# Layer 2 of a two-layer GraphSAGE stage: x·W_r computed beside x·W_l in the projection instead of inside the neighbour sums

## The reference, cut to what matters

```python
def _sage_conv(x, src, tgt, W_l, b_l, W_r):
    n = x.shape[0]
    msgs = x[src]
    agg = jax.ops.segment_sum(msgs, tgt, num_segments=n)
    deg = jax.ops.segment_sum(jnp.ones((src.shape[0],), x.dtype), tgt, num_segments=n)
    agg = agg / jnp.maximum(deg, 1.0)[:, None]
    return agg @ W_l + b_l + x @ W_r
src, tgt = (edge_index[0], edge_index[1])
h = jax.nn.relu(_sage_conv(x, src, tgt, W_l1, b1, W_r1))
logits = _sage_conv(h, src, tgt, W_l2, b2, W_r2)
```

## Time and profile before

| | us |
|---|---|
| median of 3 runs (lowest, highest) | 3331.05 (3328.54, 3333.71) |
| the profiled execution's own time | 3306.88 |
| its span, from first to last instruction | 3304.9 |
| TensorE busy in the span | 2592.2 (78%) |
| VectorE busy | 1966.1 (59%) |
| GpSimd busy | 1819.5 (55%) |
| ScalarE busy | 773.9 (23%) |
| sums of layer 1 | 1913 to 2469 |
| `stage_project` | 2469 to 2511 |
| sums of layer 2 | 2511 to 3069 |

### The profile page before, as it was taken

One profiled execution on the slowest core, in us unless ns is written; L12 is line 12 of the kernel. 1 busy time (PEld: TensorE's weight loads), 2 busy tenths in 40 slices (PEclk: granted clock), 3 DMA queues, 4 the chain that ended last, 5 costly groups with the idle time before them and its releaser, 6 DMA issues. The chain is left out here.

```text
span 3304.9 us, 33972 instructions
## 1 busy us (share of the span) xinstructions
PE 2592.2 (78%) x8449; PEld 1445.8 (44%) x8449; DVE 1966.1 (59%) x4316; ACT 773.9 (23%) x2022; POOL 1819.5 (55%) x1847
## 2 busy tenths in 40 slices
PE   4487784199999899879999877777777777777598
PEld 1133331055544444446666644433334343443476
DVE  7999996377776667514333644444435444444768
ACT  1001010277666666522232300000001000000132
POOL 3777777476665556412100067777754777777310
PEclk8788897599999999989999977788868877777799
DMA  9222220499999999961110033333343333334311
GB/s 256 68 69 82 61 81 13 149 264 263 255 239 234 221 235 234 189 163 49 40 39 9 13 106 105 105 105 105 106 89 101 106 106 105 105 105 103 86 50 41
DMA packets 198569, 401.32 MB, mean 121 GB/s; under 512 B 44315, under 2 KB 93230, under 8 KB 198064
## 3 DMA queue, kind: packets, MB, share of 16 engines
q0 software_dynamic: 93888, 248.27, 31.0%
q1 hardware_dynamic: 98672, 145.05, 13.7%
q10 hardware_dynamic: 5826, 5.93, 0.6%
HBM read 296.76 MB, written 104.52 MB: 121 GB/s over the span
## 5 line engine op out<-in xcount | busy, mean ns | idle before, releaser
L1492 POOL DMA_INDIRECT nbr_yg<-y_d,gidx x878 | 830.1, 945 | 273.0 <-PE nbr_sum L1555 143.6
L1555 PE MATMUL nbr_sum<-nbr_yg,nbr_hot 128*128 128x258 f32 x1756 | 735.3, 534 | 287.3 <-DMA nbr_yg<-y_d,gidx 228.6
L1518 DVE TENSOR_TENSOR nbr<-nbr_sum,nbr 128x258 f32 x878 | 373.5, 425 | 613.4 <-PE nbr_sum L1555 546.7
L1555 PEld LDWEIGHTS nbr_sum<-nbr_yg,nbr_hot 128*128 128x128 f32 x1756 | 367.0, 246 | 643.4 <-DMA nbr_yg<-y_d,gidx 237.7
L704 POOL DMA_INDIRECT qg<-q_d,rb x480 | 470.7, 981 | 322.0 <-DVE hb L787 200.8
L818 PE MATMUL p_sum<-hb,wide 128*96 128x512 f32 x960 | 470.1, 604 | 58.0 <-ACT hb L747 57.1
L362 POOL DMA_INDIRECT recs_d<-recs,slot_src x416 | 403.5, 970 | 152.9 <-issue 135.2
L787 DVE TENSOR_TENSOR hb<-p_h,qg 128x512 f32<-128x512 f32 x480 | 318.3, 684 | 167.1 <-DMA qg<-q_d,rb 156.7
L747 ACT ACTIVATE hb<-hb 128x512 f32<-128x512 f32 x480 | 298.6, 630 | 285.5 <-DVE hb L787 277.5
L566 PE MATMUL acc<-col_hot,lane_hot 128*128 128x440 f16 x832 | 209.9, 419 | 126.8 <-DVE lane_hot L521 126.7
L818 PEld LDWEIGHTS p_sum<-hb,wide 128*96 128x96 f32 x960 | 149.8, 164 | 239.7 <-issue 110.8
(11 more groups left out here) (277 smaller groups left out, 3108.4 us busy)
## 6 DMA issues: line engine op xcount, KB each, us to landing
agg_d<-agg SPq DMA_DIRECT2D x240, 192.4 KB, 5.8
nbr_yg<-y_d,gidx POOLq DMA_INDIRECT x878, 2.7
p_low<-p_d SPq DMA_DIRECT2D x11, 768.0 KB, 13.1
recs_d<-fill SPq DMA_DIRECT2D x16, 510.0 KB, 17.4
rb<-recs_d SPq DMA_DIRECT2D x60, 136.0 KB
qg<-q_d,rb POOLq DMA_INDIRECT x480
recs_d<-recs,slot_src POOLq DMA_INDIRECT x416
agg_d<-no_sums SPq DMA_DIRECT2D x1, 6540.8 KB, 58.5
```

The costliest lines, as they stand in the source:

```text
L1492: pool.indirect_dma_start(yg[t % YB][:, 0:D], None, S.y[:, :], bass.IndirectOffsetOnAxis(ap=C.gidx[:, t:t + 1], axis=0)).then_inc(s_gath[t ...
L1518: dve.tensor_tensor(nbr, p_sum[t % SUMS][:, 0:W], nbr, ALU.add).then_inc(s_acc, 1)
L1555: pe.matmul(p_sum[t % SUMS][:, 0:W], hot[t // BT % HOTS][:, t % BT, :], yg[t % YB][:, :], start=True, stop=True).then_inc(s_sum, 1)
```

## The change

The products x·W_r and the bias of layer 2 leave `stage_neighbours(..., 1)`. `stage_project` loads W_l and W_r side by side into one tile `w_lr` of 512 columns, and for each node tile its two matmuls are 512 columns wide and fill a whole PSUM bank: y in columns 0 to 255, z in columns 256 to 511. A third matmul adds the bias to the right half. VectorE copies the left half out as before; ScalarE copies the right half to `C.z` in a new step `kept`, which waits for `out.empty`, that is for VectorE's copy of the same bank. In ScalarE's order `kept(t - 1)` stands between the relu of tile t+1 and the turned copy of tile t. TensorE waits for `s_z` besides `out.empty` before it fills a bank again. Layer 1 is as it was.

```diff
--- before.py
+++ after.py
@@ -1371,18 +1371,20 @@
     with ExitStack() as ctx:
         m = Mem(nc, ctx, "project_")
         HB, XB, YB = 3, 3, 4
-        w_l, rdeg = m.sb("w_l", [P, KD, D]), m.sb("rdeg", [P, NT, 1])
+        w_lr, b_r, rdeg = m.sb("w_lr", [P, KD, 2 * D]), m.sb("b_r", [1, D]), m.sb("rdeg", [P, NT, 1])
         h = [m.sb(f"h{b}", [P, D]) for b in range(HB)]
         x = [m.sb(f"x{b}", [P, D]) for b in range(XB)]
         y = [m.sb(f"y{b}", [P, D]) for b in range(YB)]
         tr, out = Ring(m, "turn", 3), Ring(m, "out", 3)
-        s_w, s_deg, s_h, s_x = (m.sem(n) for n in ("w", "deg", "h", "x"))
+        s_w, s_deg, s_h, s_x, s_z = (m.sem(n) for n in ("w", "deg", "h", "x", "z"))
         s_yst = [m.sem(f"yst{b}") for b in range(YB)]
 
         with nc.Block() as block:
             @block.sync
             def _(sp):
-                sp.dma_start(w_l[:, :, :], rows_on_partitions(A.W_l2)).then_inc(s_w, 16)
+                sp.dma_start(w_lr[:, :, 0:D], rows_on_partitions(A.W_l2)).then_inc(s_w, 16)
+                sp.dma_start(w_lr[:, :, D:2 * D], rows_on_partitions(A.W_r2)).then_inc(s_w, 16)
+                sp.dma_start(b_r[:, :], A.b2.rearrange("(a n) -> a n", a=1)).then_inc(s_w, 16)
                 for t in range(NT):
                     sp.wait_ge(out.empty, t + 1)
                     sp.dma_start(S.y[t * P:(t + 1) * P, :], y[t % YB][:, :]).then_inc(s_yst[t % YB], 16)
@@ -1423,13 +1425,20 @@
                         act.wait_ge(tr.full, t - XB + 1)
                     act.activation(x[t % XB][:, :], h[t % HB][:, :], ACT.Relu).then_inc(s_x, 1)
 
+                def kept(t):
+                    act.wait_ge(out.empty, t + 1)
+                    act.activation(C.z[:, t, :], out.banks[t % len(out.banks)][:, D:2 * D], ACT.Copy).then_inc(s_z, 1)
+
                 relu(0)
                 for t in range(NT):
                     if t + 1 < NT:
                         relu(t + 1)
+                    if t > 0:
+                        kept(t - 1)
                     src = tr.take(act, t)
                     act.activation(C.xT[:, :, t * P:(t + 1) * P], src[:, 0:KD * P].rearrange("p (k n) -> p k n", n=P),
                                    ACT.Copy).then_inc(tr.empty, 1)
+                kept(NT - 1)
 
             @block.tensor
             def _(pe):
@@ -1440,24 +1449,26 @@
                         last = pe.transpose(dst[:, k * P:(k + 1) * P], x[t % XB][:, k * P:(k + 1) * P], C.ident[:, :])
                     last.then_inc(tr.full, 1)
 
-                pe.wait_ge(s_w, 16)
+                pe.wait_ge(s_w, 48)
                 transposes(0)
                 for t in range(NT):
                     if t + 1 < NT:
                         transposes(t + 1)
                     pe.wait_ge(tr.empty, t + 1)
+                    if t >= len(out.banks):
+                        pe.wait_ge(s_z, t - len(out.banks) + 1)
                     dst = out.fill(pe, t)
                     for k in range(KD):
-                        last = pe.matmul(dst[:, 0:D], C.xT[:, k, t * P:(t + 1) * P], w_l[:, k, :], start=(k == 0),
-                                         stop=(k == KD - 1))
-                    last.then_inc(out.full, 1)
+                        pe.matmul(dst[:, :], C.xT[:, k, t * P:(t + 1) * P], w_lr[:, k, :], start=(k == 0), stop=False,
+                                  skip_group_check=True)
+                    pe.matmul(dst[:, D:2 * D], C.ones[0:1, :], b_r[:, :], start=False, stop=True,
+                              skip_group_check=True).then_inc(out.full, 1)
         m.clear_sems()
 
 
 def stage_neighbours(nc, C, A, S, layer):
 
 
-    W_r = A.W_r1 if layer == 0 else A.W_r2
     with ExitStack() as ctx:
         m = Mem(nc, ctx, f"nbr{layer}_")
         BT = 8
@@ -1478,8 +1489,9 @@
         with nc.Block() as block:
             @block.sync
             def _(sp):
-                sp.dma_start(w_r[:, :, :], rows_on_partitions(W_r)).then_inc(s_w, 16)
-                sp.dma_start(b_r[:, :], (A.b1 if layer == 0 else A.b2).rearrange("(a n) -> a n", a=1)).then_inc(s_w, 16)
+                if layer == 0:
+                    sp.dma_start(w_r[:, :, :], rows_on_partitions(A.W_r1)).then_inc(s_w, 16)
+                    sp.dma_start(b_r[:, :], A.b1.rearrange("(a n) -> a n", a=1)).then_inc(s_w, 16)
 
             @block.gpsimd
             def _(pool):
@@ -1495,7 +1507,7 @@
 
             @block.scalar
             def _(act):
-                for tile in range(NT):
+                for tile in range(NT if layer == 0 else 0):
                     act.wait_ge(s_z, tile + 1)
                     act.activation(C.z[:, tile, :], p_z[:, 0:D], ACT.Copy).then_inc(s_z_taken, 1)
 
@@ -1545,7 +1557,7 @@
                 pe.wait_ge(s_zero, YB)
                 for t in range(NTILE):
                     tile, at = divmod(t, EVERY)
-                    if at % (EVERY // KD) == EVERY // KD - 1 and tile < NT:
+                    if layer == 0 and at % (EVERY // KD) == EVERY // KD - 1 and tile < NT:
                         product(tile, at // (EVERY // KD))
                     if t % BT == 0:
                         pe.wait_ge(s_hot, t // BT + 1)
```

## The result

The changed kernel is slower: 3394.21 us median (3389.48 to 3398.89), the kernel before 3332.38 (3328.54 to 3335.52) beside it, a ratio of 1.0191 with a 95% interval of [1.0169, 1.0214]. The medians are 61.8 us apart (1.0186), where 58.8 were forecast (3390 us).

The account below looks back on a forecast made before the run. The prediction took GpSimd's gather issuing to bound the sums and tile-by-tile handovers the projection. It added 55.9 + 0.6 + 2.3 + 0 = +58.8 us to the 3331.05 us median: 3390 us, range 3376 to 3414.

Parts of the forecast that it names:

- The sums of layer 2 give back nothing: Sums of layer 2: removing 63.9 us of TensorE work beside GpSimd's issuing changes 0 us, bounds -3 to +3.
- The products, 2.50 us a tile: Projection: a tile's 512-column products with the bias matmul last 2.50 us where they lasted 1.13.
- The ring, 3.70 us a turn: Projection: products, VectorE's copy, ScalarE's copy of z, turned copy and next products follow without overlap, 3.70 us a tile.
- The cold start, +2.3 us: Projection's first tile: products at clock 0.50 take 4.84 us in place of 2.50, bounds 0 and 4.7.
- The loads, +0.6 us: Projection's start: TensorE's first transposes wait for three loads in place of one, +0.6 us.
- the last products and copy: Projection's end, after 24 turns: last products 2.50 us, 0.04 to VectorE's copy, and that copy 0.42.
- The open ring: Rival, projection: ScalarE's copy of z is not in the way, a tile every 2.66 us, 3365 us; chance 0.05.
- sums bound by TensorE: Rival, sums of layer 2: the products' 63.9 us come off, 3326 us; chance 0.02.
- The falling clock: Rival, projection: TensorE's clock swings to 0.50 half of the time, 21 us more, 3411 us; chance 0.18.
- The PSUM rule: Projection: two engines may not read one bank at once, so copies take turns; otherwise 0.45 us a turn, 10.8 us less.

Follow-up runs that it names:

- the kernel with the two steps swapped: Changed kernel with ScalarE making the turned copy of tile t ahead of the copy of z of tile t-1; 1.0081 of the kernel before.
- VectorE's copies: Changed kernel with the copy of z moved from ScalarE to VectorE, right behind its copy of y; 1.0081 of the kernel before.
- the readers in the other order: Changed kernel with ScalarE copying z as soon as the products are done and VectorE copying y after it; 1.0140 of the kernel before.
- the ring of narrow products: Kernel before, 256-column products and z in the sums, with only ScalarE's new copy step and TensorE's wait for it added; 1.0100 of the kernel before.

## Why the prediction was right, point by point

- *The sums of layer 2 give back nothing.* Right on the chip of the forecast: 558.5 us against 558.4, with TensorE's clock down to 0.64. Shown by the stages. On chips with late gathers the cover is thinner than "nothing, -3 to +3": removing the work gives some 10 us of 640 (shown by the stages of six profiles; the two ratios alone reach to 1.000 and beyond).
- *The products, 2.50 us a tile.* They last 2.61. The first 512-column record starts after a wait, and the bias matmul follows 1.92 us later and not 1.81; in the kernel with the two steps swapped, where TensorE doesn't wait, it is 1.81 again. The earlier trace rows were taken from a stretch without a wait in front.
- *The ring, 3.70 us a turn.* Right in every link, mis-sized by 0.12: 0.11 of it the products, 0.02 the turned copy (0.38 us for 0.36), less 0.01 in the steps between. Over 24 turns it is +2.8 us. That it is a ring is shown by three kernels: the swap (2.71), VectorE's copies (2.72) and the readers in the other order (3.36).
- *The cold start, +2.3 us.* The first turn took 4.88 us in place of 3.82, +1.1 us: the clock rose within the first products. In the second profile of the same kernel it was 6.2 us, over three turns, past the upper bound of 4.7. The single value has no meaning finer than that.
- *The loads, +0.6 us.* 0.9: from the projection's first load to TensorE's first products 4.86 us, before 3.94.
- *The sum.* 24 turns without the clock 91.6, the cold start 1.1, the last products and copy 3.1, less 35.9, and 0.9 for the loads: +60.8 us, the whole of the difference in the profiles. The forecast's errors partly cancel: +2.8 for the ring, -1.2 for the cold start, +0.3 for the loads and +0.1 at the end. Since the cold start alone moved by 5 us between two profiles, that the sum came within 2 us of the profiles and 3 of the medians is in part luck. The forecast's own bounds, added up with the 5 us for the spread, give 3377 to 3403 and not 3379 to 3400; its stated range, 3376 to 3414, spans both.
- *The rivals.* The open ring and sums bound by TensorE are refuted. The falling clock did not come in this kernel, after the first tiles: TensorE waited 0.84 us in every turn and the clock stayed at 1.00, so a pause near the forecast's "about a microsecond" in every tile did not bring it down here. But the ring of narrow products ran at 0.50 from end to end, so its 18% were not idle. The swinging that the Trainium skill describes ("TensorE: Matmul & The Clock Gate", "A second HAM failure mode: psum-queue depth-cycling") was seen in neither ring: one stayed at 1.00, the other at 0.50. In the sums the clock does go back and forth between the levels; that TensorE's pauses there are the cause is not shown.
- *The PSUM rule.* The forecast set 10.8 us for VectorE's copy in the ring. The readers in the other order kept them apart and took it out: 0.46 us a turn, 11 us. The rule of the Trainium skill, "PSUM — Partial Sum Buffer", "Terms", costs taking turns, but not which turn comes first. That both read at the same time wasn't tried.

## What to carry to other kernels

Work that lies beside a bound engine is free where it is, or nearly so (of 64 us, 0 to 11 came back when it went); moved to a stage in which engines hand over tile by tile, it costs its full length. Before adding a copy to an idle engine, look at what stands behind it in that engine's order: if that is the input of the engine whose result the copy waits for, a pipeline becomes a ring, and swapping two instructions opens it. Of the 60.8 us here, 26 were the ring (103.1 less 77.1 us) and 35 the wider products with their bias and loads.

## What the runs showed of the hardware that was not expected

- Busy share doesn't tell the clock. TensorE is busy 78% in the wide ring at a granted clock of 1.00, and 75% in the narrow ring at 0.50, in rows of the same form. Records at 0.50 are longer, so a low clock fills its own busy share.
- The gap of 0.30 us behind an indirect gather is the same with a semaphore wait and an empty instruction in it as without them.
- The same program takes 3334 us on one chip and 3622 on another; in the sums a gather takes 1.25 us of the pace on the one and 1.43 on the other.
